# The norm's root on GpSimd, one selection matmul, and the next attention's first scores and exponentials moved ahead of the entropy model's last steps

## The chip, the cores and the metric

One core of one Trainium2 chip. The metric is the device time of one execution in microseconds (us); less is better.

## The reference

`x` is 8 images of 192 channels by 4096 pixels, float32. Two layers follow, each of the form x = x + f(groupnorm(x)) with 32 groups of 6 channels:

```python
# layer 0: a non-local attention in each image
q = prelu(w1 x + b1, a1); k = prelu(w2 x + b2, a2)   # 24 channels
v = prelu(wa x + ba, aa)                             # 192 channels
out = softmax(q^T k over keys) v                     # 4096 x 4096 scores
# layer 1: an entropy model in each channel, at x - 0.5 and x + 0.5
for i in range(4):                                   # 1 -> 3 -> 3 -> 3 -> 1
    logits = softplus(m[i]) @ logits + b[i]
    if i < 3: logits = logits + tanh(f[i]) * tanh(logits)
likelihood = max(|sigmoid(sign*upper) - sigmoid(sign*lower)|, 1e-6)
```

A group norm's scale is 1 / sqrt(variance + 1e-5).

## The kernel before, in words

The program is written out by hand, one instruction stream for each engine; nothing but semaphores orders one stream against another, and each stream runs in the order in which it stands. Each image b has a **phase B** (attention) and, behind it, a **phase A**, in which the entropy model of image l and the projections (q, k, v) of image l + 1 are interleaved. The order is: a first phase A with projections alone (`l is None`), phase B of image 0, seven turns of a loop with phase A (l, with projections) and phase B (l + 1), and a last phase A without projections.

**Phase B.** 8 blocks (`j`) of 512 queries, each in 16 steps (`p`) of 256 keys. In a step PE makes two score matmuls (`scores`, L1117) for step p + 2 and 24 matmuls that sum the values (L1344, L1346, L1348); ACT makes two exponentials of the scores, one to float16 (`e_hi`, L613) and one to float32 (`e_32`, L616); DVE takes their difference (`low`, L1016, `e_lo`). PE waits for `full_ready` before the scores and for `lo_ready` before the sums. In the last block stands the first norm of the image after (`gn1`, the helper `chain`, L777): DVE sums up statistics, PE averages over groups (`averages1`, L1081), DVE writes the variance `gvar` (L795), ACT takes the root (`deviation1`, L591, behind its exponentials of p = 5), DVE inverts, makes one Newton step (L798 to L802) and scales the projection weights (L811) at p = 8; PE's `shifts` (L1099) waits for that at p = 9.

**Phase A.** First DVE adds attention's last block to x and takes its statistics (L891, L893). Then the second norm (`gn2`, same helper) goes through DVE, PE and ACT (`deviation2`, L595). Its result `rsnm` (scale and shift of each channel) is spread over the 128 partitions by six small matmuls with `sel_sb` (L1260), and DVE makes from it the scales and `biases` of the entropy model (L836 to L849). The 14 first **banks** of the projections stand around it: PE fills one of two banks (`qk_bank`, L1161, 8 of them; `value_bank`, L1172), ACT writes its negative part (`negative`, L637), DVE combines (`value`, L925, and for q and k `low_part`, L932), and GpSimd casts (`queries`, L544, `values`, L551, L553). PE may fill bank n only when DVE has read bank n - 2. ACT's order is three negatives, the root, two negatives, the wait for `biases`, then `first_tanh` (L649) and `negative` in turns; PE's is banks 0 to 2, first average, bank 3, second average, bank 4, the six selection matmuls, then the rest.

Then come 48 slots `s`. In each, PE makes the first and second layer (L1200, L1214), ACT the tanh of both (L656) and the input's tanh of slot s + 4, and DVE the gates (L949). Every fourth slot has the third layer (L1142), `logits` (L903), sums on GpSimd, and `halves` and `size` on ACT (L622, L627). Slots 0 to 10 also carry the ten last value banks; slots 11 to 42 a score matmul each for the maxima of attention's first block (L1184, L1006). At the end of slot 43 DVE splits the maxima in six small steps (`split_max`, L864 to L869), PE transposes them (`turn_max`, L1105) at the end of its slot 44, DVE copies them (`rows_out`, L876) and SP writes them into `qst` (L359), which the first scores need (`max_in`). After slot 47 PE makes `scores(0, 0)` and `scores(0, 1)`, ACT `exps` 0 and 1 behind its last tanh, and DVE `low` 0 as the first thing of phase B.

`arena` holds three input slots of the entropy model (`t0`), and in phase B `e_hi`, `e_lo` and `e_32` over the same words.

Of the kernel before, what the change touches and what calls it, by code (L numbers as in the profile page):

```python
# [5 lines left out]
ALU = mybir.AluOpType  # L6
# [65 lines left out]
GN1_STEPS = 13  # L72
# [47 lines left out]
def program(nc, x, wall, cols, g6, sel, eye, diag, mraw, fraw, braw, x2d, out):  # L120
    x_rows = x.rearrange("b c h w -> (b c) (h w)")
    out_rows = out.rearrange("b c h w -> (b c) (h w)")
    with ExitStack() as ctx:
# [15 lines left out]
        sel_sb = sb("sel_sb", [HALF, PER_H, P])  # L139
# [7 lines left out]
        gstd = sb("gstd", [HALF, 2])  # L147
# [6 lines left out]
        gstd2 = sb("gstd2", [HALF, 2])  # L154
        rstd2 = sb("rstd2", [HALF, 2])
        tmp_a2 = sb("tmp_a2", [HALF, 2])
        tmp_b2 = sb("tmp_b2", [HALF, 2])
        rsnm = sb("rsnm", [HALF, 2, 2])
        statc = sb("statc", [P, PER_H, 4])
# [35 lines left out]
        e_hi = arena[:, 0:4 * N].bitcast(F16).rearrange("p (s n) -> p s n", s=4)  # L195
        e_lo = arena[:, 4 * N:8 * N].bitcast(F16).rearrange("p (s n) -> p s n", s=4)
        e_32 = arena[:, 8 * N:12 * N].rearrange("p (s n) -> p s n", s=2)
# [96 lines left out]
        def _(sp):  # L294
# [4 lines left out]
            for dst, src in ((eye_sb[:, :], eye), (msp, mraw), (gates[:, :, :], fraw), (diag_sb, diag), (bra, braw),  # L299
                             (sel_sb[:, :, :], sel)):  # L300
                sp.dma_start(dst, src).then_inc(consts_in, 16)
# [139 lines left out]
        def _(pool):  # L441
            for counted in (out_norm, out_turn, x2_ready, *stored):
                pool.sem_inc(counted, START)
            pool.memset(xp[HALF:HALF + 1, 1, :], 1.0).then_inc(set_gp, 1)
# [87 lines left out]

            def phase_a(l, proj):
# [28 lines left out]
                if proj:  # L562
                    for n in range(QK):
# [13 lines left out]
            def phase_b(l):  # L577
                for u in range(UNITS - LATER, UNITS):
                    sums(l, u)
                    difference(l, u)  # L580

            phase_a(None, True)
            coefficients()
            with pool.Fori(0, B - 1) as l:
# [5 lines left out]
        def _(act):  # L590
            def deviation1(b):  # L591
                act.wait_ge(gn1_step, b * GN1_STEPS + 6)
                act.activation(gstd[:, :], gvar[:, :], ACT.Sqrt).then_inc(gn1_std, 1)

            def deviation2(l):  # L595
                act.wait_ge(gn2_step, l * GN2_STEPS + 6)
                act.activation(gstd2[:, :], gvar2[:, :], ACT.Sqrt).then_inc(gn2_std, 1)

# [30 lines left out]
            def phase_a(l, proj):  # L629
# [45 lines left out]
                deviation2(l)  # L675
                if proj:
                    for n in range(3, 5):
                        negative(n)
                act.wait_ge(gn2_step, l * GN2_STEPS + 16)
                for i in range(LEAD):  # L680
                    first_tanh(i)
                    if proj:
                        negative(5 + i)
                if proj:
                    for n in range(5 + LEAD, QK + V_LEAD):
# [744 lines left out]
```

## Time and profile before

| what | us |
|---|---|
| median of 3 runs | 4978.88 |
| lowest and highest run | 4977.02, 4981.09 |
| the profiled execution's own time | 4973.9 |
| its span, first to last instruction | 4972.1 |
| PE busy | 4497.8 (90%) |
| DVE busy | 4219.2 (85%) |
| ACT busy | 3645.1 (73%) |
| POOL (GpSimd) busy | 712.9 (14%) |

The span is that of the profiled execution, which was 5.0 us under the median. Shares are means over phase B, in which PE has hardly a gap, and phase A, in which the engines wait for each other in turns. A matmul's record is modelled at its end, so the starts are what to compare.

### The profile page before, as it was taken

Reading aid. Unit: us, or ns where it says so; the run is one execution under the profiler, and the core shown is the slowest. Engines: PE = TensorE matmul, PEld = TensorE weight load, DVE = VectorE, ACT = ScalarE, POOL = GpSimd, SP = SyncE. Lnnn points to the kernel's source line nnn. Section 1 sums busy time; section 2 is a strip of 40 time slices with the busy share of each in tenths; the row PEclk is TensorE's granted clock in tenths of the full one; section 3 lists DMA queues with packets and bytes.
Section 4 is the critical chain, followed back from the end, with each engine's and each line's share of the span. In section 5 each row is a group of like instructions: output and inputs, shape, how many; then the busy total and the mean of one; then the engine's idle time right before and its main releaser. Section 6 shows DMA issues by size and latency. Waiting matters only on the chain.

```text
span 4972.1 us, 106254 instructions
## 1 busy us (share of the span) xinstructions
PE 4497.8 (90%) x38408; PEld 2992.0 (60%) x38408; DVE 4219.2 (85%) x5586; ACT 3645.1 (73%) x4008; POOL 712.9 (14%) x751
## 2 busy tenths in 40 slices
PE   6999889998899988999789997999979998899976
PEld 4887338872478724886258862588616785177831
DVE  6997789978899788996889968899698996989866
ACT  3666877768767697676877679776796777966788
POOL 4200301003010130101200012000220102101012
PEclk9999999999999999999999999999999999999998
DMA  3001431014201142011420024110241112310133
GB/s 79 17 14 32 111 79 30 25 40 114 76 23 31 36 121 67 23 31 49 115 60 29 25 59 116 49 33 21 71 109 44 33 29 73 103 50 23 33 83 97
DMA packets 154988, 280.18 MB, mean 56 GB/s; under 512 B 37441, under 2 KB 37825, under 8 KB 152706
## 3 DMA queue, kind: packets, MB, share of 16 engines
q1 hardware_dynamic: 154434, 272.94, 21.1%
q8 instruction: 330, 5.41, 0.5%
q14 instruction: 224, 1.84, 0.1%
HBM read 205.49 MB, written 50.33 MB: 51 GB/s over the span
## 4 chain that ended last, share of the span: by engine, by line
PE 54%; DVE 17%; ACT 14%; issue 13%; DMA 1%; SPq 1%; DVEq 0%; POOL 0%; ACTq 0%; POOLq 0%
PE ps L1344 10%; PE ps L1346 10%; PE ps L1348 10%; PE ps L1117 7%; PE ps L1296 6%; ACT th L656 6%; DVE mxp L1021 5%; ACT arena L649 4%; DVE th L949 4%; DVE arena L1016 3%; PE ps L1214 3%; PE ps L1200 2%; PE ps L1172 2%; PE ps L1142 1%; PE ps L1161 1%
## 5 line engine op out<-in xcount | busy, mean ns | idle before, releaser
L1344 PE MATMUL ps<-v_sb,arena 128*128 128x193 f16 x8192 | 2020.7, 247 | 13.0 <-DVE arena L1016 13.0
L1346 PE MATMUL ps<-v_sb,arena 128*128 128x192 f16 x8192 | 2029.7, 248 | 0.0
L1348 PE MATMUL ps<-v_sb,arena 128*128 128x193 f16 x8192 | 2012.8, 246 | 0.0
L613 ACT ACTIVATE arena<-ps 128x1024 f16<-128x1024 f32 x1024 | 1050.6, 1026 | 899.0 <-PE ps L1117 898.9
L1016 DVE TENSOR_TENSOR arena<-arena 128x1024 f16<-128x1024 f32 x1024 | 1295.6, 1265 | 240.1 <-ACT arena L616 240.0
L1021 DVE TENSOR_REDUCE mxp<-ps 128x1 f32<-128x512 f32 x1792 | 1178.2, 687 | 50.0 <-PE ps L1296 40.3
L949 DVE SCALAR_TENSOR_TENSOR th<-th,gates,ps 128x1024 f32<-128x1024 f32 x768 | 951.6, 1277 | 183.0 <-ACT th L656 177.0
L616 ACT ACTIVATE arena<-ps 128x1024 f32<-128x1024 f32 x1024 | 1046.2, 1022 | 0.2 <-DVE arena L1016 0.2
L1346 PEld LDWEIGHTS ps<-v_sb,arena 128*128 128x128 f16 x8192 | 796.0, 97 | 262.2 <-issue 0.3
L656 ACT ACTIVATE th<-ps,biases 128x1024 f32<-128x1024 f32 x768 | 825.9, 1114 | 150.4 <-PE ps L1200 87.0
L1344 PEld LDWEIGHTS ps<-v_sb,arena 128*128 128x128 f16 x8192 | 793.4, 97 | 145.5 <-issue 19.6
L1348 PEld LDWEIGHTS ps<-v_sb,arena 128*128 128x128 f16 x8192 | 808.4, 99 | 0.5
L1296 PE MATMUL ps<-kst,qst 128*128 128x512 f16 x1792 | 679.6, 379 | 40.9 <-DVE mxp L1021 35.3
L1117 PE MATMUL ps<-qst,kst 128*128 128x512 f16 x2048 | 612.0, 381 | 17.7 <-ACT arena L616 15.3
L1214 PE MATMUL ps<-th,w 64*64 64x512 f32 x3072 | 434.0, 634 | 157.8 <-DVE th L949 153.2
L649 ACT ACTIVATE arena<-x,biases,scl 128x1024 f32<-128x1024 f32 (+1 forms) x400 | 496.1, 1241 | 4.6 <-DVE biases L844 3.9
L1200 PE MATMUL ps<-arena,w1s 64*64 64x512 f32 x3072 | 437.5, 638 | 64.9 <-DVE th L949 24.5
L524 POOL TENSOR_TENSOR lu<-lu 128x512 f32<-128x512 f32 x96 | 122.0, 1271 | 2180.7 <-ACT lu L622 2180.7
L1214 PEld LDWEIGHTS ps<-th,w 64*64 64x64 f32 x3072 | 97.8, 137 | 339.6 <-issue 339.3
L1200 PEld LDWEIGHTS ps<-arena,w1s 64*64 64x64 f32 x3072 | 93.1, 136 | 341.4 <-issue 322.0
L1117 PEld LDWEIGHTS ps<-qst,kst 128*128 128x128 f16 x2048 | 189.5, 98 | 95.0 <-ACT arena L616 20.1
L544 POOL CAST shared<-lu 128x512 f16<-128x512 f32 x64 | 61.1, 955 | 1217.3 <-DVE lu L925 1217.3
(122 smaller groups left out, 3294.6 us busy)
## 6 DMA issues: line engine op xcount, KB each, us to landing
x<-x2d SPq DMA_DIRECT2D x1152, 64.0 KB, 2.4
arena<-x2d SPq DMA_DIRECT2D x768, 64.0 KB, 2.5
xp<-x_dram SPq DMA_DIRECT2D x18, 1536.0 KB, 12.6
shared<-x_dram SPq DMA_DIRECT2D x64, 384.0 KB, 3.6
x2d<-shared SPq DMA_DIRECT2D x64, 384.0 KB, 3.0
res<-x2d SPq DMA_DIRECT2D x96, 256.0 KB
out_dram<-res SPq DMA_DIRECT2D x96, 256.0 KB
kst<-shared SPq DMA_DIRECT2D x32, 256.0 KB, 4.8
```

The costliest lines, as they stand in the source:

```text
L613: act.activation(e_hi[:, q % 4, :].rearrange("p (k n) -> p k n", k=2), sc, ACT.Exp)
L616: act.activation(e_32[:, q % 2, :].rearrange("p (k n) -> p k n", k=2), sc, ACT.Exp).then_inc(full_ready, 1)
L649: ins = act.activation(t0[lo:hi, v % T0R, d, :], x4[lo:hi, v % X4R, :], ACT.Tanh, bias=biases[lo:hi, d, 0, u:u + 1], scale=scl[lo:hi, u:u ...
L656: act.activation(dst, ps[:, at:at + 2, :], ACT.Tanh, bias=biases[:, d, layer, u:u + 1]).then_inc(after, 1)
L949: dve.scalar_tensor_tensor(t, t, gates[:, c // 4, col:col + 1], ps[:, at:at + 2, :], ALU.mult, ALU.add).then_inc(after, 1)
L1016: dve.tensor_tensor(e_lo[:, q % 4, :], e_32[:, q % 2, :], e_hi[:, q % 4, :], ALU.subtract).then_inc(lo_ready, 1)
L1021: dve.tensor_reduce(mxp[:, m // BLOCKS, m % BLOCKS:m % BLOCKS + 1], ps[:, bank + m % 2, :], AX_X, ALU.max).then_inc(max_red, 1)
L1117: ins = pe.matmul(ps[:, 2 * (q % 2) + i, :], kst[:, m * P:(m + 1) * P], qst[:, q_col:q_col + N], start=True, stop=True)
L1296: pe.matmul(ps[:, bank + m % 2, :], qst[:, q_col + m // BLOCKS * P:q_col + (m // BLOCKS + 1) * P], kst[:, (m % BLOCKS) * N:(m % BLOCKS + 1 ...
L1344: pe.matmul(acc, eh, v_sb[:, m, 0:C + 1], start=(m == 0 and t % 2 == 0), stop=False, skip_group_check=True)
L1346: pe.matmul(acc[:, 0:C], eh, v_sb[:, m, VW:VW + C], start=False, stop=False, skip_group_check=True)
L1348: ins = pe.matmul(acc, el, v_sb[:, m, 0:C + 1], start=False, stop=(m == MT - 1), skip_group_check=True)
```

## The change

- **Root.** The two ACT square roots and DVE's reciprocal and the sqrt's buffers are gone. GpSimd raises the variance to the power -0.5 (`root1`, `root2`), and DVE makes the same Newton step on it. `root2` stands behind `queries(0)` in GpSimd's stream, `root1` at the end of its phase B. In attention's last block the rest of the chain (Newton step and weights) moves from p = 8 to p = 7. Each chain has one DVE step less; `gn2` writes the power straight into `rsnm`, so that a copy goes too.
- **Selection.** Six matmuls of 4 columns become one of 24 columns; ahead of it DVE spreads `rsnm` with one multiplication (`own`). The constant `sel` is smaller.
- **Order at the second norm.** PE: banks 0 and 1, both averages, bank 2, selection, the rest. DVE: statistics, `query(0)`, three parts of the chain up to `own`, `query(1)`, the rest of the chain, then `query(2)` on. ACT: three negatives, the wait for `biases`, then tanh and negative in turns.
- **Order in the slots.** ACT's `negative` of a value bank stands ahead of the input's tanh and of `halves` and `size`. `turn_max` stands right behind PE's first layer of slot 44, ahead of the second; `rows_out` one slot earlier.
- **Attention's start.** `scores(0, 0)` stands in slot 47 between first and second layer, `scores(0, 1)` in slot 48 ahead of the second; `exps` 0 and 1 ahead of ACT's tanh of the second layer in the same slots, `low` 0 ahead of DVE's last gate. In `arena` `e_32` is now first, then `e_hi`, `e_lo`.

```diff
+            def root1(i):
+                if i is None:
+                    pool.wait_ge(gn1_step, 6)
+                else:
+                    spread = pool.compute_val(i * GN1_STEPS + 6)
...
+                pool.tensor_tensor(rstd[:, :], gvar[:, :], minus_half[:, :], ALU.pow).then_inc(gn1_std, 1)
+            def root2(l):
...
+                pool.tensor_tensor(rsnm[:, :, 0], gvar2[:, :], minus_half[:, :], ALU.pow).then_inc(gn2_std, 1)
...
                 if proj:
-                    for n in range(QK):
+                    queries(0)
+                root2(l)
+                if proj:
+                    for n in range(1, QK):
                         queries(n)
...
-                deviation2(l)
-                if proj:
-                    for n in range(3, 5):
-                        negative(n)
                 act.wait_ge(gn2_step, l * GN2_STEPS + 16)
                 for i in range(LEAD):
                     first_tanh(i)
                     if proj:
-                        negative(5 + i)
+                        negative(3 + i)
...
+                    if proj and s >= SLOTS - 1:
+                        exps(pj(BLOCKS * PAIRS, 0), s - SLOTS + 1)
                     if 1 <= s <= SLOTS:
...
                         tanh("h2", c, th2[:, c % HR2, :, :], 2, h2_mm, t2_ready)
+                    if proj and s >= 1 and s - 1 + V_LEAD < VB:
+                        negative(QK + s - 1 + V_LEAD)
                     if s + LEAD < SLOTS:
                         first_tanh(s + LEAD)
...
-                dve.wait_ge(std, std_now)
-                step(dve.reciprocal(r[:, :], dev[:, :]))
-                step(dve.tensor_tensor(a[:, :], r[:, :], r[:, :], ALU.mult))
+                dve.wait_ge(root, root_now)
+                step(dve.tensor_tensor(a[:, :], r, r, ALU.mult))
...
+                step(dve.tensor_tensor(own[:, :, :], sel_sb[:, P:].unsqueeze(2).to_broadcast(shape),
+                                       rsnm.rearrange("p h k -> p (h k)").unsqueeze(1).to_broadcast(shape), ALU.mult))
...
-                        if last and p in (2, 4, 6, 8, 10):
+                        if last and p in (2, 4, 6, 7, 10):
                             next(chain1)
...
                     qk_bank(0)
                     qk_bank(1)
-                    qk_bank(2)
                 averages2(l, 0)
-                if proj:
-                    qk_bank(3)
                 averages2(l, 1)
                 if proj:
-                    qk_bank(4)
+                    qk_bank(2)
                 pe.wait_ge(gn2_step, l * GN2_STEPS + 12)
-                for q in range(PER_H):
-                    ins = pe.matmul(ps[:, 6, 4 * q:4 * q + 4], sel_sb[:, q, :],
-                                    rsnm.rearrange("p h k -> p (h k)"), start=True, stop=True)
-                ins.then_inc(gn2_mm, 1)
+                pe.matmul(ps[:, 6, 0:4 * PER_H], sel_sb[:, 0:P], own.rearrange("p q k -> p (q k)"), start=True,
+                          stop=True).then_inc(gn2_mm, 1)
...
+                    if proj and s == FIRST_AT + MAXES + 1:
+                        turn_max(pj(BLOCKS, 0), 0)
+                    if proj and s == SLOTS - 1:
+                        pe.wait_ge(max_in, pj(BLOCKS * 16, 16))
+                        scores(0, 0)
+                    if proj and s == SLOTS:
+                        pe.wait_ge(h1_ready, l * SLOTS + SLOTS)
+                        scores(0, 1)
                     if l is not None:
                         if 1 <= s <= SLOTS:
                             second_layer(s - 1)
```

## Rows read from the trace of the kernel before

**Rows 1.** The page: span, and busy time of each engine
```profile
span 4972.1 us, 106254 instructions
PE 4497.8 (90%) x38408; PEld 2992.0 (60%) x38408; DVE 4219.2 (85%) x5586; ACT 3645.1 (73%) x4008; POOL 712.9 (14%) x751
```

**Rows 2.** Windows: length, busy PE, PEld, DVE, ACT, POOL, granted clock, DMA
```profile
706.00:1085.00 379.00, 370.79 (x3595) 306.65 (x3591) 337.31 (x472) 263.16 (x298) 26.18 (x17) 1.00 0.10 27
1085.00:1120.70 35.70, 30.67 (x105) 17.51 (x104) 21.76 (x46) 18.39 (x26) 13.05 (x16) 0.86 0.23 66
1120.70:1306.30 185.60, 152.44 (x1059) 45.48 (x1059) 161.09 (x173) 164.76 (x168) 42.87 (x44) 0.96 0.41 105
```

**Rows 3.** Timeline (start, length), phase B's last block, ACT and DVE
```profile
1057.44 1.28 ACT L593 ACT_TABLE_LOAD   x1
1058.60 0.15 DVE L795 TENSOR_SCALAR gvar<-ps 96x2 f32<-96x2 f32 x1
1058.78 0.20 ACT L593 ACTIVATE gstd<-gvar 96x2 f32<-96x2 f32 x1
1059.00 1.28 ACT L613 ACT_TABLE_LOAD   x1
```

**Rows 4.** Timeline of the same stretch, PE; in brackets the idle time before
```profile
1059.84 0.59 PE L1117 MATMUL ps<-qst,kst 128*128 128x512 f16 x2
1062.29 0.60 PE L1117 MATMUL ps<-qst,kst 128*128 128x512 f16 x2
...
1065.57 0.59 PE L1117 MATMUL ps<-qst,kst 128*128 128x512 f16 x2
...
1067.03 1.24 PE L1099 MATMUL ps<-w_s,gmean 96*1 96x320 f32 x4 [0.87 <-DVE w_s L811]
1070.21 0.59 PE L1117 MATMUL ps<-qst,kst 128*128 128x512 f16 x2
```

**Rows 5.** One line's instructions on POOL: shortest, median, longest in ns
```profile
L465 POOL TENSOR_TENSOR th<-th x30: 213/218/1127, 99.3 to 131.4; 128x12 f32<-128x12 f32 x30
```

**Rows 6.** Timeline, second norm and projections of image 1
```profile
1096.22 1.97 PE L1161 MATMUL ps<-xp,w_s 96*128 96x512 f32 x4
...
1098.99 0.15 DVE L795 TENSOR_SCALAR gvar<-ps 96x2 f32<-96x2 f32 x1
...
1103.38 1.28 ACT L649 ACT_TABLE_LOAD   x1 [2.30 <-DVE biases L844]
...
1104.68 2.49 ACT L649 ACTIVATE arena<-x,biases,scl 48x1024 f32<-48x1024 f32 x2
...
1105.75 5.61 PE L1161 MATMUL ps<-xp,w_s 96*128 96x512 f32 x8 [0.73 <-DVE lu L925]
...
1120.71 1.09 PE L1200 MATMUL ps<-arena,w1s 64*64 64x512 f32 x8
```

**Rows 7.** Timeline, second norm of the last image
```profile
4759.62 2.72 PE L1260 MATMUL ps<-rsnm,sel_sb 96*128 96x4 f32 x12 [1.85 <-DVE rsnm L833]
```

**Rows 8.** Timeline, slots with value banks
```profile
540.15 1.57 PE L1172 MATMUL ps<-w_s,xp 96*128 96x192 f32 x8 [1.71 <-DVE lu L925]
...
543.22 2.12 ACT L656 ACTIVATE th<-ps,biases 128x1024 f32<-128x1024 f32 x2 [0.33 <-PE ps L1200]
```

**Rows 9.** Timeline, slots 43 to 48 and the start of phase B
```profile
680.69 1.09 PE L1214 MATMUL ps<-th,w 64*64 64x512 f32 x8 [0.70 <-DVE th L949]
...
682.90 0.24 PE L1105 MATMUL ps<-eye,mparts 128*12 128x128 f16 x1 [1.12 <-DVE mparts L869]
682.98 2.47 DVE L949 SCALAR_TENSOR_TENSOR th<-th,gates,ps 128x1024 f32<-128x1024 f32 x2
...
698.68 1.23 DVE L1016 TENSOR_TENSOR arena<-arena 128x1024 f16<-128x1024 f32 x1 [0.55 <-ACT arena L616]
```

**Rows 10.** Windows of PE alone, behind `turn_max`: busy, granted clock, DMA
```profile
1293.60:1297.00 3.40, 3.40 (x17) 0.55 0.20 58
2517.30:2520.70 3.40, 3.04 (x25) 1.00 0.21 58
```

More of the change, by code:

```diff
@@ L158, in program @@
         rsnm = sb("rsnm", [HALF, 2, 2])
+        own = sb("own", [HALF, PER_H, 4])
+        minus_half = sb("minus_half", [HALF, 2])
         statc = sb("statc", [P, PER_H, 4])
@@ L580, in phase_b @@
                     difference(l, u)
+                root1(pool.compute_val(l + 2))
+            root1(None)
             phase_a(None, True)
             coefficients()
+            root1(1)
             with pool.Fori(0, B - 1) as l:
@@ L682, in phase_a @@
                     if proj:
-                        negative(5 + i)
+                        negative(3 + i)
                 if proj:
-                    for n in range(5 + LEAD, QK + V_LEAD):
+                    for n in range(3 + LEAD, QK + V_LEAD):
                         negative(n)
@@ L706, in phase_a @@
                             size(l, u)
-                    if proj and s >= 1 and s - 1 + V_LEAD < VB:
-                        negative(QK + s - 1 + V_LEAD)
-                if proj:
-                    exps(pj(BLOCKS * PAIRS, 0), 1)
             def phase_b(b, l):
@@ L775, in softplus, with chain @@
                 yield
-            def chain(step_sem, base, n, mm, mm_base, std, std_now, stats, m, mean, var, dev, r, a, b):
+            def chain(step_sem, base, n, mm, mm_base, root, root_now, stats, m, mean, var, r, a, b):
                 def step(ins):
@@ L828, in step @@
                     dve.wait_ge(gn2_step, base + n[0])
[L830 to L833 removed]
+                yield from chain(gn2_step, base, n, gn2_mm, l * 3, gn2_std, l + 1, stats2, mv2, gmean2, gvar2,
+                                 rsnm[:, :, 0], tmp_a2, tmp_b2)
+                step(dve.scalar_tensor_tensor(rsnm[:, :, 1], gmean2[:, :], -1.0, rsnm[:, :, 0], ALU.mult, ALU.mult))
+                shape = [HALF, PER_H, 4]
+                step(dve.tensor_tensor(own[:, :, :], sel_sb[:, P:].unsqueeze(2).to_broadcast(shape),
+                                       rsnm.rearrange("p h k -> p (h k)").unsqueeze(1).to_broadcast(shape), ALU.mult))
                 yield
@@ L912, in result, with low @@
                                          ).then_inc(res_ready, 1)
+            def low(pairs, q):
+                dve.wait_ge(full_ready, pairs + (q + 1))
+                dve.tensor_tensor(e_lo[:, q % 4, :], e_32[:, q % 2, :], e_hi[:, q % 4, :],
+                                  ALU.subtract).then_inc(lo_ready, 1)
             def phase_a(l, proj):
@@ L966, in phase_a @@
                     next(weights)
+                    low(0, 0)
                     return
@@ L970, in phase_a @@
                 add_half(l, BLOCKS - 1, 1)
-                if proj:
-                    query(0)
                 seen = dve.compute_val(l * 2 * BLOCKS + 2 * BLOCKS)
@@ L977, in phase_a @@
                 if proj:
+                    query(0)
+                next(chain2)
+                next(chain2)
+                next(chain2)
+                if proj:
                     query(1)
@@ L980, in phase_a @@
                 if proj:
-                    query(2)
-                next(chain2)
-                next(chain2)
-                if proj:
-                    query(3)
-                next(chain2)
-                if proj:
-                    for n in range(4, QK + V_LEAD):
+                    for n in range(2, QK + V_LEAD):
                         query(n)
@@ L993, in phase_a @@
                         gate("h1", s, th1[:, s % HR1, :, :], F1O, t1_ready, h1_ready)
+                    if proj and s == SLOTS:
+                        low(pj(BLOCKS * PAIRS, 0), 0)
                     if 1 <= s <= SLOTS:
@@ L1022, in reduce @@
                                       AX_X, ALU.max).then_inc(max_red, 1)
-                low(dve.compute_val(b * BLOCKS * PAIRS), 0)
                 for j in range(BLOCKS):
```

61 lines of the change are left out of this document (20 added, 41 removed).

## The prediction

> **What bounds the kernel now.** I read the page first: PE is busy for 90% of the span, DVE for 85%, ACT for 73%, GpSimd hardly [rows 1]. Then windows by stage for one image. In phase B PE is busy for 370.8 of 379 us, so that only a stop of PE itself counts there. In the stretch from attention's end to the first layer of slot 0 PE is busy for 30.7 of 35.7 us at a mean clock of 0.86, and in the 48 slots no engine is full (PE 82%, DVE 87%, ACT 89%): there the order of the streams counts [rows 2]. So each edit is priced where it stands, and each place recurs 7 or 8 times.
>
> **Root of the first norm, phase B's last block (8 times).** ACT loads a table (1.28 us), waits for the variance, takes the root (0.20) and loads the old table again (1.28), until 1060.28; its exponentials had ended at 1057.4, so they come 2.9 us late [rows 3]. PE shows the price a little later. Its score matmuls start 2.45 us apart (1059.84, 1062.29), then 3.28 apart (1065.57): 0.84 us lost. From there to the next step's at 1070.21 are 4.64 us, of which 2.45 are a step and 1.24 the weight shifts; 0.95 are left, and the bracket names DVE's weights, which the late chain delivered at p = 8 [rows 4]. With the root on GpSimd the tables never change (exponential and tanh already follow each other with no load in the slots), and with the chain at p = 7 the weights are ready one step before PE asks. Both stops go: 1.8 us, 8 times, **-14.4**. What is late next: DVE's chain (five small steps and two scalings, some 1.7 us) now stands ahead of `low` 9, and DVE has 2.45 us in a step of which `low` takes 1.23; the surplus is about 0.5 us, less than the lead that DVE has over PE. I cost it at nothing; without that lead it would be 0.5 us a time.
>
> **The power on GpSimd.** No row has it. The nearest on that engine are small multiplications, 0.21 us in the median and 1.13 at the longest [rows 5]. I take 0.6 us, the middle, since a power of two elements is more than a product and the instruction is small. Between the variance at 1058.60 [rows 3] and its use at p = 7 lie some 2.4 us, so in phase B even 2 us would be hidden. GpSimd's queue at that time is empty: `root1` stands behind the sums of blocks 0 to 5, and `root2` behind one cast that waits for nothing new.
>
> **Second norm beside projections (7 times).** The first tanh of the entropy model starts at 1104.68, 5.7 us after the variance. Earlier by: one bank less ahead of the first average, 1.8 us (1.97 with its tail), and no bank between the averages, of whose 1.97 us DVE's small steps cover most, so 0.5; the table load right ahead of the tanh, 1.28 [rows 6]. Reciprocal and copy go and `own` comes, 0.1 less. The power costs 0.6 for 0.20, and 0.1 more for the hand over. The six selection matmuls are worth nothing here, as DVE is in `query` meanwhile. Sum: the tanh starts 3.2 us sooner (2.6 to 4). But banks 3 and 4 are no longer behind us by then. Eleven banks instead of nine follow the first tanh, and the first layer of slot 0 stands behind all of them: today at 1120.71, 16.0 us after the tanh [rows 6]. Two more banks are 3.4 to 3.6 us at full clock. The chain is shorter and PE is the bound, so the net is +0.2 us. At half clock a bank costs up to 1.7 us more (two banks took 5.61 us across a change of clock [rows 6]); the new order has PE waiting for DVE between banks 2, 3 and 4, and I add 0.2. Seven times 0.4: **+3** (-7 to +13).
>
> **The last image.** No banks stand there and the chain is bare: its selection takes 2.72 us [rows 7]. One matmul of six leaves about 0.5, so -2.2; `own` and the slower power give back 0.7, the copy and the reciprocal 0.3: **-1.8** (its tanh has no table load in the way, that one is hidden behind the selection). At the program's start the power costs **+0.3**.
>
> **Negatives earlier (7 times).** In a slot with `halves` PE waits 1.71 us for DVE's reading of a value bank, but ACT, the fullest engine there, then stands only 0.33 us [rows 8]. The work of ACT is the same, so I give it 0.5 us for an image, two such slots and their like: **-3.5** (0 to -7).
>
> **Attention's start (7 times).** Two edits act against each other. PE now waits for `split_max` ahead of the second layer of slot 43, which starts today at 680.69, while `turn_max` can't start before 682.90. DVE is in `split_max` till then anyway, and the two gates behind it start at 682.98, the second at about 684.2; with the second layer behind `turn_max` (1.09 us, then a tanh of 1.1) that gate can't start before 685.5. The chain from there on runs 1.4 us late. On the other side `low` 0 now waits for exponentials that stand behind ACT's last tanh, and starts at 698.68 [rows 9]; with them ahead, it follows DVE's gate of slot 46, itself held back by 1.9 us as two exponentials push its tanh. That makes it 1.4 us sooner. Sum **0**, from -1.4 to +1.4 each, 7 times. `qst`'s rows leave some 3 us earlier and are no wait; the smaller `sel` and the moved arena cost nothing, since the same waits cover them.
>
> **Sum.** -14.4 + 3 - 1.8 + 0.3 - 3.5 + 0 = -16.4 us. The profiled execution took 4973.9, which gives 4957.5; it stands 5.0 under the median of the runs, 4978.88, so the time to expect is **4962 us**. A measurement of this kernel tells a difference of about 0.2%, 10 us, from none.
>
> **Rivals.** *More comes out (0.20).* The `turn_max` wait is taken up by slack on ACT (it has no input tanh from slot 44 on), and the exponentials' 1.4 us stay: 7 x 1.4 = 10 us more, 4952; with good luck at the banks 4944. For it: ACT is idle in those slots. Against: DVE and the tiles pass the delay on one by one.
>
> *Little comes out (0.25).* Phase B gives 14.4, and the seven transitions take back a good part: 1 us each at the two places gives -14.4 - 5 + 14 = -5, about 4973. For it: the eleven banks are PE's own work, and the power may take 1.1 us instead of 0.6, which is 0.5 x 7 by itself.
>
> *Slower (0.09): PE's clock during the banks.* Place: from the first average to the first layer of slot 0. Today the mean clock there is 0.86 [rows 2], and the half clock falls where ACT sets the pace (tanh of 2.49 us and a negative for each bank), so it costs little. With PE idle between banks 1 and 4 it can fall later or longer, into the last eleven banks, at 1.7 us a bank. It takes 4 us an image, two to three banks at 1.2 GHz, to eat the gain and 10 us more: 7 x 4 = 28, 4990. The same end would come from a power of over 3 us, for which no row speaks.
> The clock after a wait can be read at `turn_max`: after PE's wait of 1.12 us [rows 9] the next 3.4 us had a mean clock of 0.55 in one image and 1.00 in another [rows 10]. So such a wait brings the half clock (1.2 GHz) in some images and not in others. The new order makes PE's wait there longer, about 3.3 us with the idle time ahead of it. *Half clock in all seven (0.10, inside the forecast's range):* 3.4 us at half clock are at most 1.7 us of PE's work, and DVE and ACT cover part of it; at 1 us in each of the four images that would not have had it, 4966. The Trainium skill ("TensorE: Matmul & The Clock Gate", section "What's actually happening") has it that the slow clock is the default and only activity lifts it; by that rule a longer wait makes this case the likely one. The trace agrees as far as 0.55 behind a wait goes, and not with it as a certainty, by the 1.00.
>
> **How the numbers follow.** The forecast's own case (0.46, the all-half-clock one in it) spans 4955 to 4968.8, all of it over 10 us below 4978.9. With the rivals beside it the range is 4944 to 4977. Faster by over 0.2%: 0.46 + 0.20 = 0.66; within: 0.25; slower: 0.09.
>
> **What would show it.** Right: no table load on ACT in the loop; score matmuls 2.45 us apart through phase B's last block, but for the shifts; the first tanh about 3 us sooner after attention's end and the first layer of slot 0 at 35.5 to 36.5 us; in slot 43 the second layer behind `turn_max`; `low` 0 at the same distance from `turn_max` as now, 15.8 us. Wrong: a power over 1.5 us, a mean clock under 0.8 between attention's end and slot 0, or phase B's last block still with a gap.

## The result, and the profile of the changed kernel

| kernel | median of the runs, us | lowest and highest | profiled execution, its span |
|---|---|---|---|
| before | 4977.95 (4 runs) | 4963.69, 4981.09 | 4973.9, 4972.1 |
| changed | 4924.10 (4 runs) | 4923.73, 4931.16 | 4923.73, 4921.9 |

The ratio is 0.9905 with a 95% interval of 0.9891 to 0.9918: the change saves 54 us, faster by more than 0.2%. The forecast was 4962 (4944 to 4977), a saving of 16; the sign was right, the size was not, and the result lies 20 us below the range.

The page of the changed kernel, against [rows 1]:

```profile
span 4921.9 us, 106055 instructions
PE 4466.4 (91%) x38328; PEld 2971.3 (60%) x38328; DVE 4210.8 (86%) x5569; ACT 3598.8 (73%) x3958; POOL 724.6 (15%) x769
```

Windows by stage for the same image, against [rows 2] (length, busy PE, PEld, DVE, ACT, POOL, granted clock, DMA):

```profile
695.41:1074.41 379.00, 372.34 (x3608) 307.22 (x3607) 338.30 (x473) 262.17 (x296) 26.86 (x18) 1.00 0.10 28
1074.41:1109.76 35.35, 28.22 (x95) 16.14 (x95) 21.77 (x45) 15.87 (x23) 13.73 (x17) 0.90 0.23 66
1109.76:1296.07 186.31, 152.94 (x1064) 44.90 (x1064) 161.91 (x174) 169.29 (x174) 42.88 (x44) 0.97 0.46 113
```

PE is busy for 31 us less, and ACT for 46, of which 42 are its table loads (36 of them before, 3 now, none in the loop). The 50.2 us between the spans were mostly waits of PE and stretches at its lower clock. I cut both traces at the same events and took the difference in each piece, summed over the images. Here "the slots" go from the first layer of slot 0 to the first value sum of phase B.

| piece | before, us | changed, us | difference |
|---|---|---|---|
| phase B, first image | 378.01 | 376.32 | -1.7 |
| phase B, seven others, mean | 384.86 | 381.71 | -22.1 |
| attention's end to the first layer of slot 0, seven, mean | 35.57 | 35.79 | +1.5 |
| the slots, seven, mean | 190.14 | 186.32 | -26.7 |
| last image and start | | | -1.2 |

The transition (attention's end to slot 0) came out as forecast in its sum, but not evenly: it is 2.3 us shorter behind image 0 (34.99 to 32.71) and 0.6 us longer in the mean of the other six. Two pieces did not come out: I had given the slots 3.5 us, and phase B 14.4 of its 23.8.

**Phase B's last block.** The timeline of the changed kernel (start, length), against [rows 3] and [rows 4]:

```profile
1049.80 0.15 DVE L799 TENSOR_SCALAR gvar<-ps 96x2 f32<-96x2 f32 x1
1050.10 0.70 POOL L540 TENSOR_TENSOR rstd<-gvar,minus_half 96x2 f32<-96x2 f32 x1 [92.20 <-DVE gvar L799]
...
1053.48 0.59 PE L1121 MATMUL ps<-qst,kst 128*128 128x512 f16 x2
...
1055.92 0.59 PE L1121 MATMUL ps<-qst,kst 128*128 128x512 f16 x2
...
1056.44 1.24 PE L1103 MATMUL ps<-w_s,gmean 96*1 96x320 f32 x4
...
1059.62 0.60 PE L1121 MATMUL ps<-qst,kst 128*128 128x512 f16 x2
```

The scores are 2.44 us apart, and 3.70 across the shifts (one step and 1.24): both stops are gone. The power takes 0.70 us, where I took 0.6.

**The slots.** One edit works at two places there. Before, slots 7 and 8 and slot 11 of image 1, in brackets the idle time before:

```profile
1147.07 1.05 ACT L622 ACTIVATE lu<-lu 128x1024 f32<-128x1024 f32 x1
...
1148.54 0.48 ACT L637 ACTIVATE lu<-ps 128x384 f32<-128x384 f32 x1
...
1149.81 2.21 PE L1172 MATMUL ps<-w_s,xp 96*128 96x192 f32 x8 [1.71 <-DVE lu L925]
...
1151.95 1.98 PE L1200 MATMUL ps<-arena,w1s 64*64 64x512 f32 x8
...
1154.00 2.14 ACT L656 ACTIVATE th<-ps,biases 128x1024 f32<-128x1024 f32 x2 [1.46 <-PE ps L1200]
...
1167.06 1.06 ACT L622 ACTIVATE lu<-lu 128x1024 f32<-128x1024 f32 x1 [1.10 <-POOL lu_sign L518]
...
1168.54 0.47 ACT L637 ACTIVATE lu<-ps 128x384 f32<-128x384 f32 x1
...
1169.88 0.61 PE L1184 MATMUL ps<-kst,qst 128*128 128x512 f16 x1 [5.52 <-DVE lu L925]
```

Changed:

```profile
1136.24 1.06 ACT L635 ACTIVATE lu<-lu 128x1024 f32<-128x1024 f32 x1
...
1136.93 1.57 PE L1176 MATMUL ps<-w_s,xp 96*128 96x192 f32 x8
...
1139.24 1.09 PE L1204 MATMUL ps<-arena,w1s 64*64 64x512 f32 x8 [0.73 <-DMA arena<-x2d]
...
1151.82 0.49 ACT L650 ACTIVATE lu<-ps 128x384 f32<-128x384 f32 x1
...
1154.19 1.06 ACT L635 ACTIVATE lu<-lu 128x1024 f32<-128x1024 f32 x1 [0.76 <-POOL lu_sign L518]
...
1154.36 0.61 PE L1188 MATMUL ps<-kst,qst 128*128 128x512 f16 x1 [2.91 <-DVE lu L936]
```

Before, ACT's negative of the last value bank (1168.54) stands behind `halves` (1167.06), and that waits for GpSimd. So PE is without work for 5.52 us ahead of the first score of the maxima; changed, the negative is done before `halves` begins, and 2.91 us are left. The smaller wait, 1.71 us in slot 7, is gone. Behind it PE's clock fell to 1.2 GHz in five of the seven images (windows of PE before and after, same columns as in [rows 10]):

```profile
1152.00:1155.40 3.40, 3.40 (x20) 0.71 0.30 89
```

```profile
1135.00:1141.00 6.00, 5.24 (x41) 1.00 0.70 160
```

The first layer at 1151.95 took 1.98 us instead of 1.09, and ACT stood 1.46 us for it. From the first layer of slot 0 to the first maximum it was 49.2 to 49.5 us in those five images, 48.2 and 47.7 in the two where the clock did not fall there, and 44.6 in the changed kernel. So some 1.3 us x 5 of this belong to the clock and 3.4 us x 7 to the waits themselves, 30 in all. From the first maximum to `turn_max` the changed kernel then took 125.1 us instead of 124.3, 5.4 more in seven images, and from there to the first value sum 2.3 less, which gives the 26.7. The kernels below with the same order in that middle piece took 124.3 to 125.4 there, so the 5.4 are no effect of an edit that these runs can show.

**Phase B's first step.** Before, image 1 to 2, timeline and windows of PE:

```profile
1309.45 0.60 PE L1117 MATMUL ps<-qst,kst 128*128 128x512 f16 x2 [2.15 <-ACT arena L616]
...
1310.89 0.24 PE L1344 MATMUL ps<-v_sb,arena 128*128 128x193 f16 x1 [0.84 <-DVE arena L1016]
```

```profile
1311.00:1314.40 3.40, 3.40 (x23) 0.50 1.02 226
```

Changed, image 0 to 1:

```profile
689.03 0.60 PE L1121 MATMUL ps<-qst,kst 128*128 128x512 f16 x2 [1.21 <-DVE th L960]
...
692.84 0.24 PE L1345 MATMUL ps<-v_sb,arena 128*128 128x193 f16 x1 [1.64 <-DVE arena L922]
```

```profile
692.80:696.20 3.40, 3.32 (x34) 1.00 1.05 246
```

Phase B used to begin at 1.2 GHz in seven images of seven, and its second step came 5.71 to 6.03 us after the first; now this is so in one of seven, and in the other six it comes after 4.39 to 4.50. That is the rest of phase B: 6 x 1.6 = 9.6 us, beside 8 x 1.8 = 14.4 for the last block. One image of seven is partly luck of this execution: in six kernels below with the same streams at this place (e1, e4, e5, e6, e9, e12) phase B begins at 1.2 GHz in one to four images of seven, 16 of 42.

### The profile page after: what moved, and what is told of

Read it like the earlier page. It is cut to its first block, busy times and chain, and to the rows that moved or that the text cites. A ratio compares the mean times of both kernels' runs of the same rounds, so it can differ in the third digit from the quotient of the medians.

```text
span 4921.9 us, 106055 instructions
## 1 busy us (share of the span) xinstructions
PE 4466.4 (91%) x38328; PEld 2971.3 (60%) x38328; DVE 4210.8 (86%) x5569; ACT 3598.8 (73%) x3958; POOL 724.6 (15%) x769
## 4 chain that ended last, share of the span: by engine, by line
PE 57%; DVE 16%; ACT 12%; issue 12%; DMA 1%; SPq 1%; DVEq 0%; POOL 0%; ACTq 0%; POOLq 0%
PE ps L1345 10%; PE ps L1347 10%; PE ps L1349 10%; PE ps L1121 7%; PE ps L1297 6%; ACT th L669 6%; DVE mxp L1026 5%; ACT arena L662 4%; DVE arena L922 3%; DVE th L960 3%; PE ps L1218 3%; PE ps L1204 3%; PE ps L1176 2%; PE ps L1165 2%; PE ps L1146 2%
## 5 line engine op out<-in xcount | busy, mean ns | idle before, releaser
L1297 PE MATMUL ps<-kst,qst 128*128 128x512 f16 x1792 | 679.8, 379 | 40.3 <-DVE mxp L1026 34.1
L1121 PEld LDWEIGHTS ps<-qst,kst 128*128 128x128 f16 x2048 | 188.8, 97 | 93.8 <-DVE th L960 14.5
L650 ACT ACTIVATE lu<-ps 128x384 f32<-128x384 f32 (+1 forms) x192 | 102.6, 534 | 177.6 <-PE ps L1165 120.3
```

The costliest lines, as they stand in the source:

```text
L1121: ins = pe.matmul(ps[:, 2 * (q % 2) + i, :], kst[:, m * P:(m + 1) * P], qst[:, q_col:q_col + N], start=True, stop=True)
L1297: pe.matmul(ps[:, bank + m % 2, :], qst[:, q_col + m // BLOCKS * P:q_col + (m // BLOCKS + 1) * P], kst[:, (m % BLOCKS) * N:(m % BLOCKS + 1 ...
```

## The experiments

Each was timed against the kernel before on its own chip, four chips in all. The median of the kernel before was 4973.26 for e1 to e4, 4970.69 for e5 to e8, 4973.04 for e9 to e11 and 4967.54 for e12. Differences between two changed kernels are given by the medians; by the ratios, which take the chip out, they come out up to 4 us otherwise, and what decides is whether the intervals of the ratios overlap.

**e1, the negatives back.** ACT's `negative` of a value bank behind `halves` and `size` again, all else changed.

```diff
-                    if proj and s >= 1 and s - 1 + V_LEAD < VB:
-                        negative(QK + s - 1 + V_LEAD)
                     if s + LEAD < SLOTS:
                         first_tanh(s + LEAD)
...
                         if (s - 5) % 4 == 3:
                             size(l, u)
+                    if proj and s >= 1 and s - 1 + V_LEAD < VB:
+                        negative(QK + s - 1 + V_LEAD)
```

> The changed kernel with one edit undone: ACT's negative of a value bank stands again behind the input's tanh, halves and size of its slot. Theory A (the order of ACT in the value-bank slots is worth about 3.3 us an image, because PE waits for the bank that DVE could not read): slots 7 to 12 get longer by 2 to 4 us in each of the 7 images, the run takes 4924 + 23 = 4947 us (4941 to 4952). Theory B (the slots got shorter through the state in which the faster second norm leaves clock and queues, not through this order): 4924 +- 4 us, slots as in the changed kernel.

4946.53 us, ratio 0.9945 (0.9931 to 0.9959): 22.4 us above the changed kernel. The wait of 1.71 us is back in seven images, the one at slot 11 is 5.33 to 5.44, and the first maximum comes 49.0 to 49.1 us after slot 0 in six images. The slots take 189.8 us instead of 186.3, which is 24.5 in seven images. Theory A was right.

**e9, the negatives between.** The same `negative` behind the input's tanh, ahead of `halves`.

> The changed kernel, with ACT's negative of a value bank behind the input's tanh, but still ahead of the halves and the size of the entropy model. Theory A: the wait of 1.71 us that PE had for DVE's reading of a value bank comes from the halves and the size that stood ahead of the negative; with those behind it the wait is gone and the clock stays at 2.4 GHz in slots 6 to 13. The time stays within 5 us of the changed kernel's 4924, and the slots 7 to 13 keep their length. Theory B: the tanh of 2.2 us ahead of the negative is enough to make PE wait, so the time goes towards the 4947 that the kernel with the old place gave, 4936 or more, and stretches at 1.2 GHz come back in slots 6 to 13.

4919.41 us, ratio 0.9889 (0.9874 to 0.9904), as fast as the changed kernel (the intervals overlap). The wait at slot 11 is 2.85 us and that of 1.71 is gone in all seven. So it is `halves` and `size` (and through `halves` GpSimd) that made PE wait, not the tanh.

**e2, `turn_max` back** behind the second layer of PE's slot 44.

```diff
-                    if proj and s == FIRST_AT + MAXES + 1:
-                        turn_max(pj(BLOCKS, 0), 0)
...
                         if s + V_LEAD < VB:
                             value_bank(s + V_LEAD)
+                        if s == FIRST_AT + MAXES + 1:
+                            turn_max(pj(BLOCKS, 0), 0)
```

> The changed kernel with turn_max back at the end of PE's slot 44. Theory A (turn_max ahead of the second layer holds the chain up by 1.2 to 2.3 us in slots 43 to 45, as its trace shows): PE is released earlier, slot 44's gates come 1 to 1.4 us sooner, phase B starts about 1 us sooner in each of 7 images, 4924 - 7 = 4917 us. Theory B (the early transposition is needed, since the first scores would otherwise wait for the maxima's rows, or the clock at phase B's start depends on it): 4924 to 4934 us, with a wait of scores(0, 0) for the DMA or half clock at phase B's start.

4904.63 us, ratio 0.9859 (0.9844 to 0.9874): 19.5 us faster than the changed kernel by the medians, 23 by the ratios, and faster than both theories said. The slots take 184.25 us instead of 186.32 (2.07 x 7 = 14.5) and phase B starts at 2.4 GHz in all seven (another 1.5); the transitions were 0.7 us longer each in the profiled execution, which was the slowest of its four runs. The row behind it, image 2, changed kernel and e2:

```profile
1279.45 0.22 PE L1109 MATMUL ps<-eye,mparts 128*12 128x128 f16 x1 [2.90 <-DVE mparts L875]
```

```profile
1281.61 0.22 PE L1109 MATMUL ps<-eye,mparts 128*12 128x128 f16 x1 [1.11 <-DVE mparts L875]
```

PE stands 2.90 us for the maxima in all seven images of the changed kernel, and 1.11 or 1.12 in e2 and before. In the 3.4 us behind it the clock fell in six images of seven, in e2 in three and before in four. And with `turn_max` back phase B never begins at 1.2 GHz: none of seven images in e2, e7, e10 and e11, beside the 17 of 49 with it early and attention's start in the new order (the changed kernel and the six above). Why the place of `turn_max` decides that, some 16 us later, no run shows.

**e3, attention's start back.** The first two scores behind the second layer of slot 48, `exps` and `low` 0 where they stood.

```diff
-                    if proj and s == SLOTS - 1:
-                        pe.wait_ge(max_in, pj(BLOCKS * 16, 16))
-                        scores(0, 0)
-                    if proj and s == SLOTS:
-                        pe.wait_ge(h1_ready, l * SLOTS + SLOTS)
-                        scores(0, 1)
...
                             second_layer(s - 1)
+                        if proj and s == SLOTS:
+                            pe.wait_ge(max_in, pj(BLOCKS * 16, 16))
+                            scores(0, 0)
+                            scores(0, 1)
```

> The changed kernel with attention's first scores, exponentials and first low back behind the last slot (turn_max stays early). Theory A (the early scores give PE other work ahead of phase B, so its first step runs at full clock, 1.6 us an image, and low 0 comes 1 to 1.5 us sooner): half clock at phase B's start in most images, 7 x (1.6 + 1.4) = 21 us more, 4945 us. Theory B (the clock at phase B's start is a matter of where the slots end in time, not of this edit): 4924 + 10 = 4934 us, with phase B's first step at full clock as in the changed kernel.

4943.71 us, ratio 0.9940 (0.9926 to 0.9953): 19.6 us above. From `turn_max` to the first sum it takes 18.18 us instead of 16.61 (7 x 1.57 = 11.0; by the whole length of the slots it is 1.25 an image, 8.8), and phase B begins at 1.2 GHz in seven of seven (383.04 instead of 381.71, 9.3 more). Theory A was right.

**e8, filler at the start.** e3 with nine matmuls of no use ahead of the first sums.

```diff
+                        if p == 0 and first and l is not None:
+                            pe.wait_ge(h2_ready, l * SLOTS + SLOTS - 1)
+                            for _ in range(9):
+                                pe.matmul(ps[:, mine, :], kst[:, 0:P], qst[:, 0:N], start=True, stop=True)
                         pe.wait_ge(lo_ready, pairs + (p + 1))
```

> e3_start_back (attention's start in the old order) and 9 matmuls of 512 float16 columns on PE (about 2 us at full clock, into a free bank, read by nobody) ahead of its wait for the first low. Theory A (the old start costs 1.6 us an image because PE waits and then runs the first step of phase B at half clock): first step at full clock in most images (second step 4.4 us behind the first instead of 5.9), 7 x 1.5 = 10 us less than e3_start_back's 4944, 4934 us (4931 to 4938). Theory B (the clock at that place is set by what lies longer before, or PE's idle time isn't its cause): 4944 +- 3 us, steps as in e3_start_back.

4940.86 us, ratio 0.9941 (0.9928 to 0.9954), 3 us below e3 by the medians and the same by the ratios. The filler and the first step behind it:

```profile
1906.85 2.10 PE L1317 MATMUL ps<-qst,kst 128*128 128x512 f16 x9
```

```profile
1908.80:1912.20 3.40, 3.40 (x35) 1.00 0.74 172
```

Work in PE's wait keeps the clock up: the second step comes after 4.39 us in six images and 4.92 in one. But phase B starts 1.1 us later each time, behind the filler, which takes most of that back. So theory A was right on the clock, and its 10 us did not come. It was the lower clock that made the first step long, and the changed kernel's order avoids it without a filler, in most images.

**e4, the banks' old order at the second norm**, with the power and the single selection matmul (PE: banks 0 to 2, average, 3, average, 4; DVE, ACT and GpSimd accordingly).

```diff
                     qk_bank(1)
+                    qk_bank(2)
                 averages2(l, 0)
+                if proj:
+                    qk_bank(3)
                 averages2(l, 1)
                 if proj:
-                    qk_bank(2)
+                    qk_bank(4)
```

> The changed kernel with the old order of banks about the second norm: PE banks 0 to 2, average, bank 3, average, bank 4, selection (still one matmul); root still on GpSimd (behind two casts). Theory A (my prediction's: the chain gains 3 us and two more banks behind it lose 3.5): first layer of slot 0 at 32 to 33 us after attention's end instead of 35.8, as the table load is gone and nine banks follow, so 7 x 3 = 21 us less, 4903 us, if ACT is what nine banks wait for. Theory B (PE's banks are the bound in either order): 35 to 36 us, 4924 +- 5 us.

4931.25 us, ratio 0.9918 (0.9904 to 0.9931): 7 us above by the medians, but the intervals overlap, so no clear difference; the 21 us that theory A wanted are ruled out. The first layer of slot 0 comes 36.6 us after attention's end instead of 35.8; image 0 is 33.92 instead of 32.71.

**e6, the long chain.** The second norm with its square root, table load, reciprocal and six selection matmuls, in the changed kernel's order of banks.

```diff
-                pool.tensor_tensor(rsnm[:, :, 0], gvar2[:, :], minus_half[:, :], ALU.pow).then_inc(gn2_std, 1)
...
+                act.activation(gstd2[:, :], gvar2[:, :], ACT.Sqrt).then_inc(gn2_std, 1)
...
+                if dev is not None:
+                    step(dve.reciprocal(r, dev))
```

> The changed kernel with the second norm's chain long again: root by ACT with its table loads and DVE's reciprocal, and six selection matmuls of 4 columns; the order of the banks stays new. Theory A (the banks on PE are the bound of that stretch, so a shorter chain is worth nothing where they stand): only the last image pays 2 to 3 us, first layer of slot 0 elsewhere within 1 us of the changed kernel's, 4924 + 5 = 4929 us (4924 to 4934). Theory B (the short chain carries the gain of the stretch): first tanh and first layer 2.5 to 3 us later in each image, 8 x 3 = 24 us more, 4948 us.

4936.94 us, ratio 0.9932 (0.9920 to 0.9945): 12.8 us above, between the two theories. The transitions take 36.70 us instead of 35.79 (6.4 in all) and the last image's 16.31 instead of 14.61 (1.7). The other 5 us I find in no one place.

These means of the transition need care. Kernels whose streams are the changed kernel's there (e1, e2, e3, e5, e8, e9, e12) have 34.8 to 36.5 us in the mean of seven, since 0 to 14 us of each transition run at 1.2 GHz. Images with the same time at 1.2 GHz (3.4 us in the transition, images 1 to 6) compare better: 35.1 in the changed kernel (34.9 to 35.4 in those like it), 35.6 and 35.8 in e4, 36.4 and 36.5 in e6. By this the shorter chain is worth about 1.3 us an image, and the new order of the banks some 0.5.

**e5, the first norm's weights at p = 8** instead of 7.

```diff
-                        if last and p in (2, 4, 6, 7, 10):
+                        if last and p in (2, 4, 6, 8, 10):
```

> The changed kernel with the rest of the first norm's chain back at p = 8 of attention's last block; the root stays on GpSimd. Theory A (my prediction's: of the 1.8 us that the last block lost, 0.95 were the wait for the weights, which a chain at p = 8 always delivers too late): score matmuls again 3.4 us apart at the shifts, 8 x 1 = 8 us more, 4932 us. Theory B (the weights were late only because the table loads had made ACT late): 4924 +- 3 us, phase B as long as in the changed kernel (381.5 us).

4921.53 us, ratio 0.9897 (0.9882 to 0.9911): no difference, as theory B had it. **e12** asks the same place from the other side: the root of the first norm alone back on ACT, weights at p = 8.

```diff
-                pool.tensor_tensor(rstd[:, :], gvar[:, :], minus_half[:, :], ALU.pow).then_inc(gn1_std, 1)
...
+                act.activation(gstd[:, :], gvar[:, :], ACT.Sqrt).then_inc(gn1_std, 1)
```

> The changed kernel, with the root of the first norm alone back on ACT (square root, its two table loads, DVE's reciprocal, and the weights at p = 8 as before); the second norm keeps its power on GpSimd. Theory A: this root was worth what its two stops in phase B's last block cost PE, 0.84 and 0.95 us in 8 blocks. Phase B then lasts 383.3 us instead of 381.5, the score matmuls are 3.28 us apart once in the last block again, and the time is 4936 to 4941. Theory B: part of the saving there has another source (the order of DVE's steps, the clock), so the last block stays short or loses only one of its two stops: 4924 to 4933.

4941.13 us, ratio 0.9944 (0.9931 to 0.9958): 17 us above. Timeline of its last block, ACT and PE:

```profile
1054.48 1.28 ACT L603 ACT_TABLE_LOAD   x1
1055.82 0.21 ACT L603 ACTIVATE gstd<-gvar 96x2 f32<-96x2 f32 x1
1056.04 1.28 ACT L619 ACT_TABLE_LOAD   x1
...
1059.33 0.60 PE L1119 MATMUL ps<-qst,kst 128*128 128x512 f16 x2
...
1062.61 0.59 PE L1119 MATMUL ps<-qst,kst 128*128 128x512 f16 x2
...
1064.07 1.24 PE L1101 MATMUL ps<-w_s,gmean 96*1 96x320 f32 x4 [0.87 <-DVE w_s L812]
...
1067.26 0.59 PE L1119 MATMUL ps<-qst,kst 128*128 128x512 f16 x2
```

3.28 and then 4.65 us apart, as before the change [rows 4]; phase B is 383.35 to 383.46 us in six images, 1.9 more than the changed kernel's usual 381.46. With e5 this says that both stops came from the root on ACT: the weights were late because the root was, not because of p = 8. That it is the two loads (2.56 us) and not the root itself (0.21 us) or DVE's reciprocal is read from these rows; no run has them apart.

**e7, filler at attention's end.** e2 with 14 matmuls without use as the first thing of PE's phase A, against the 1.2 GHz that follows PE's idle time there.

> e2_turn_back and 14 matmuls of 512 float16 columns on PE (about 3 us, into a free bank, read by nobody) right behind attention's last sum, where PE waits some 3.3 us for the last normalisation. Theory A (PE's wait there brings the half clock, and that is what makes the banks slow: image 0, without it, has its first layer at 32.7 us instead of 36 to 38): full clock behind attention's end, first layer at 32.5 to 33.5 us in all seven images, 6 x 4 = 24 us less than e2_turn_back's 4905, 4881 us (4878 to 4890). Theory B (the clock isn't what the banks wait for, or it falls later all the same): 4905 +- 4 us; if the extra matmuls hold up the transpositions, up to 7 x 1 us more.

4921.44 us, ratio 0.9901 (0.9887 to 0.9915), 17 us slower than e2 and slower than both theories said. Its timeline, with e2's for comparison below, shows why:

```profile
1077.38 3.19 PE L1250 MATMUL ps<-qst,kst 128*128 128x512 f16 x14 [3.13 <-issue]
1080.41 1.04 PE L1114 MATMUL ps<-eye_sb,o_sb 128*96 128x128 f32 x8
```

The filler did not start when attention ended but 3.1 us later, as late as the transposes did. PE waited for none of the other engines; what stands there is the jump of its loop from phase B back to phase A. Image 0, which gets to phase A without that jump, has no such gap: there the filler starts at once (0.05 us). In the changed kernel image 0 reaches slot 0 after 32.7 us, the others after 35.1 to 37.1. Two more kernels test this.

**e10, filler ahead of the jump**, and **e11, PE's loop written out**, each on e2:

```diff
                 phase_b(pe.compute_val(l + 1), l)
+                pe.wait_ge(full_ready, l * BLOCKS * PAIRS + 2 * BLOCKS * PAIRS)
+                for _ in range(14):
+                    pe.matmul(ps[:, 0, :], kst[:, 0:P], qst[:, 0:N], start=True, stop=True)
```

```diff
-            with pe.Fori(0, B - 1) as l:
+            for l in range(B - 1):
                 phase_a(l, True)
-                phase_b(pe.compute_val(l + 1), l)
+                phase_b(l + 1, l)
```

> The kernel of e2 (4904.6 us), with 14 matmuls into a bank that is free there put at the end of phase B on PE, ahead of the loop's jump. PE stands 3.1 to 3.8 us without work behind that jump in six images, and 3.4 to 6.8 us at 1.2 GHz follow. Theory A: PE's sequencer runs ahead while the matmuls last, the jump is hidden behind them, the statistics' transposes start on time and the clock stays at 2.4 GHz; from the transposes to the first layer of slot 0 it takes 27.35 us, and the time is 4880 to 4895. Theory B: the jump begins only when the last matmul is done, so the fill lengthens the stretch by its 3 us and the idle time stands behind it as before; 4905 to 4925.

> The kernel of e2 (4904.6 us), with PE's loop of seven turns written out, so that PE's stream has no jump between phase B and phase A. Theory A: the idle time of 3.1 to 3.8 us at that place in six images is the jump's; without it all of them look as image 0 does (first layer of slot 0 at 32.7 us from attention's end instead of 35 to 37), which gives 6 x 2 to 4 us: 4881 to 4893. Theory B: the idle time belongs to something else there (the fetching of new code, or a wait that the profile doesn't show), and stays or moves elsewhere: 4900 or more.

e10: 4904.06 us, ratio 0.9863 (0.9848 to 0.9878), no different from e2. e11: **4896.06 us**, ratio 0.9847 (0.9834 to 0.9861), 8.6 us below e2 by the medians (6 by the ratios), 28 below the changed kernel, the fastest of all. The intervals of e2 and e11 overlap, so this last step rests on the profile as well. PE between phase B and phase A, first e2:

```profile
1078.98 1.94 PE L1114 MATMUL ps<-eye_sb,o_sb 128*96 128x128 f32 x8 [3.79 <-issue]
```

e10:

```profile
1071.78 3.19 PE L1372 MATMUL ps<-qst,kst 128*128 128x512 f16 x14
1075.78 1.07 PE L1114 MATMUL ps<-eye_sb,o_sb 128*96 128x128 f32 x8 [0.82 <-issue]
```

e11:

```profile
1075.06 1.94 PE L1114 MATMUL ps<-eye_sb,o_sb 128*96 128x128 f32 x8 [2.35 <-ACT o_sb L616]
```

In e10 the jump is hidden but for 0.82 us, the transposes start as late as in e2 (3.3 to 3.9 us after the last sum) and run at 2.4 GHz: slot 0 is reached after 34.84 us in the mean of the six images instead of 37.10. The last image, which has the filler too, loses 1.0. These 12.6 us are in the profiled execution, which was the fastest of four (4896.55), and the median does not show them; e8, without a filler there, has 34.90 us in the same six images. Whether e10 saves anything stays open: theory A was right on the jump, theory B on the time. In e11 the idle time has another name, 2.35 us for attention's own output, and the transposes run at 1.2 GHz; slot 0 is reached after 34.30 us. Most of the distance to e2's 37.10 is the clock, as e8's 34.90 shows; at the same 3.4 us at 1.2 GHz e11 has 34.1 to 34.4 and the kernels with the jump 34.9 to 35.4, so the jump itself costs about 1 us in each of six images, as much as the idle time ahead of the transposes shrinks. That is less than the 2 to 4 us of theory A. Image 0's transition takes 1.25 us more than in e2, but its phase B 1.6 less, as in e7 and e8. Phase B takes 0.3 more in each of the others, for which I have no cause.

## Why the prediction was wrong in size

Term by term, by its own steps:

- **Phase B's last block, -14.4**: right. The undo cost 17 us, and 1.9 x 8 = 15 by the trace. One step of it was wrong: the 0.95 us at the shifts was not to be had by moving the chain to p = 7; e5 puts it back at p = 8 and loses nothing. The surplus of DVE at p = 7 showed nowhere.
- **The power, 0.6 us**: 0.70 and 0.69. No wait for it in phase B.
- **Second norm, +3 (-7 to +13)**: 1.5 us more than before in all, so right as a net, with some luck: one image won 2.3 us, six lost 0.6 each. The first tanh of image 1 came 15.64 us after attention's end instead of 19.67, 4.0 sooner for my 3.2 (3.8 in the mean of seven): the variance was known 3.3 us sooner, where I had counted 2.3 for the banks, and from there to the tanh it took 0.8 less for my 0.9. As I had said, the two banks that went behind the tanh took it back. The stretches at 1.2 GHz in it are still there (mean clock 0.90 in image 1, 0.86 before [rows 2]), and they cost more now: where a transition has 10.2 us of them it takes 36.6 to 37.1 us, and before it took 35.6 to 35.8. I had foreseen this direction with 0.2 us an image. The means of seven seem to say that the two edits only work as a pair (35.57 us with both old, 36.60 and 36.70 with one undone, 35.79 with both new), but at the same time at 1.2 GHz each is worth something by itself (e4, e6).
- **The last image, -1.8**: 16.16 to 14.62 us up to its slot 0, -1.5. Its selection takes 0.62 us instead of 2.72.
- **Attention's start, 0**: as a sum of two moves it was near (from `turn_max` to the first sum 16.61 us instead of 16.94, -2.3 in seven), and each half was sized fairly: I gave 1.4 us each; by the length of the slots e3 measured 1.25 and e2 2.07. I did not price **the clock of phase B's first step**, 1.6 us in six images, 9.6 in all, though the row needed was at hand: 1311.00 to 1314.40 at 0.50. The rivals looked for a new stretch at 1.2 GHz, and none for an old one that goes. The one on the clock behind `turn_max` came true in six images of seven: PE's wait there is 2.90 us where I had said 3.3.
- **Negatives earlier, -3.5 (0 to -7)**: this is the step that failed. It measured 22.4 us (e1; some 3 of them are phase B's first steps, slow in three images there and in one of the changed kernel). I had argued from the idle time of ACT, "the fullest engine there", in one slot of one image [rows 8], and capped the gain by its 0.33 us. Two things were missed. The wait that mattered was four slots later: 5.52 us of PE ahead of the first maximum, where ACT itself stood 1.10 us for GpSimd before `halves`, with the negative queued behind it. And image 0, which I read, is one of two where the clock did not fall after the wait of 1.71 us; in the other five it fell and cost 1.3 us more.

So I was short by 37.5 us (53.9 saved by the medians, 16.4 forecast). By the pieces of the trace 23.2 of them lie in the slots (26.7 for 3.5), 9.4 in phase B's first steps, 1.2 in the transitions and the last image together, and 3.7 are the difference between medians and profiled executions. The rival "more comes out" had the right sign and the wrong place: it counted on slack on ACT to take up the wait at `turn_max`, which costs 2 us an image (e2).

The Trainium skill's rule ("TensorE: Matmul & The Clock Gate", section "What's actually happening"), by which I had weighed a longer wait as a danger, holds here in the other direction as well: fewer and shorter waits gave clock back. The trace had 261.4 us at 1.2 GHz before and 211.3 in the changed kernel, and work without use in a wait (e8) kept the clock up. It also agrees at `turn_max`, where the clock fell behind a wait of 2.90 us in six images and behind 1.11 us in four.

## What to carry to other kernels

Price a reordering by the longest wait that it shortens on the critical engine, found by listing that engine's waits over the whole stage and over several images, not by the idle time of the engine whose stream is edited at one place; look for what stands queued behind an instruction that waits for a third engine. Where a wait of a microsecond or two stands ahead of TensorE work, read the granted clock behind it in every repetition: removing it may also remove a stretch at 1.2 GHz. Undo each part of a change that wins: here one part of the order in the slots cost 20 us, and taking it out was the cheapest gain. Before a mean over images is put down to an edit, compare images that spent the same time at 1.2 GHz, and look what the mean does in kernels that are alike at that place.

## What the runs showed of the hardware that I had not expected

- PE's loop jump: 3.0 to 3.8 us in which PE does nothing, between the last sum of phase B and the first instruction of phase A (e2, e7). Matmuls queued ahead of it hide it but for 0.82 us (e10). Without it PE waits 2.2 to 2.5 us there for attention's output (e11), so that the jump's own price is about 1 us.
- The same wait need not bring the same clock: 1.71 us of PE in slot 7 stood in all seven images before the change, and the clock fell behind it in five.
- A power of 96 x 2 float32 elements takes 0.69 to 0.70 us on GpSimd; a square root on ACT between exponentials took 1.28 + 0.21 + 1.28 us with its two table loads.
